# Selective scan: x·dt spread over the scan's partitions by one bf16 product of three stacked parts, and the inputs' front half moved an iteration ahead

## The reference

```python
u = lax.conv_general_dilated(x, conv_kernel, ...); u = silu(u)      # 3 taps, per channel
Bcoeff, Ccoeff = jnp.split(u @ W_bc + b_bc, 2, axis=-1)             # 16 each
dt = log1p(exp((u @ W_dt + b_dt) @ W_dtp + b_dtp))
alpha = jnp.exp(jnp.einsum('dn,bld->bldn', -jnp.exp(A_log), dt))
beta = jnp.einsum('bln,bld,bld->bldn', Bcoeff, x, dt)
_, hs = lax.associative_scan(_scan_op, (alpha, beta), axis=1)       # h = alpha*h + beta
y = jnp.einsum('bln,bldn->bld', Ccoeff, hs) + x * Dcoeff
```

## Time and profile before

| | before |
|---|---|
| median of 3 runs | 1733.51 us |
| the profiled execution, and its span | 1730.11 us, 1728.4 us |
| TensorE matmul busy | 1512.6 us (88%) |
| VectorE, ScalarE, GpSimd busy | 968.1, 763.4, 360.1 us |
| the scan's part of the span | about 1014 to 1404 us |
| granted TensorE clock, whole span | 0.881 |

### The profile page before, as it was taken

How to read it: one execution, slowest core, us unless ns; L and a number is a source line. 1 busy time by engine, 2 the same in 40 slices (tenths; PEclk the granted TensorE clock), 3 DMA queues, 4 the chain that set the end, 5 groups by cost and what they waited for, 6 DMA issues and landing times. The chain is left out here.

```text
span 1728.4 us, 24373 instructions
## 1 busy us (share of the span) xinstructions
PE 1512.6 (88%) x7922; PEld 806.6 (47%) x7922; DVE 968.1 (56%) x1959; ACT 763.4 (44%) x1346; POOL 360.1 (21%) x459
## 2 busy tenths in 40 slices
PE   3984899999999697799999948888989869999998
PEld 2761222323322475577777632222222236777776
DVE  4664788888886266522222643767676755122236
ACT  0210588888888221344343414444444314434442
POOL 2004222222120100300000013556555630000000
PEclk9995799999999798599999976777676758999999
DMA  4002122121220000100000000000000000000001
GB/s 84 1 1 73 54 68 66 40 71 65 74 75 12 1 1 1 16 15 15 14 1 14 1 1 1 1 1 0 0 0 1 1 14 15 1 15 15 15 7 43
DMA packets 56880, 38.45 MB, mean 22 GB/s; under 512 B 16780, under 2 KB 53464, under 8 KB 56792
## 3 DMA queue, kind: packets, MB, share of 16 engines
q1 hardware_dynamic: 54672, 37.04, 7.5%
q10 hardware_dynamic: 2120, 0.28, 0.1%
HBM read 22.23 MB, written 14.68 MB: 21 GB/s over the span
## 5 line engine op out<-in xcount | busy, mean ns | idle before, releaser
L1258 ACT ACTIVATE m_hidden<-m_pU,m_up_b 128x512 f32<-128x512 f32 x320 | 219.9, 687 | 272.3 <-PE m_pU L1395 272.0
L1013 DVE TENSOR_REDUCE at_nm<-at_mx 128x2 f32<-128x1024 f32 x256 | 303.1, 1221 | 45.6 <-PE at_mx L857 44.3
L1402 PEld LDWEIGHTS m_pD<-m_down,m_hidden 128*128 128x128 f32 x2560 | 296.9, 192 | 33.5 <-issue 33.5
L1402 PE MATMUL m_pD<-m_down,m_hidden 128*128 128x128 f32 x2560 | 297.1, 275 | 0.0
L1395 PE MATMUL m_pU<-m_xT_all,m_up 128*128 128x512 f32 x640 | 291.8, 602 | 1.1 <-PEq L1094 1.1
L959 ACT ACTIVATE at_probs<-at_ring 128x512 f32<-128x512 f32 x512 | 268.2, 601 | 45.3 <-PE at_ring L869 44.5
L1371 DVE TENSOR_TENSOR m_out_b<-m_pD,m_down_b 128x512 f32<-128x512 f32 x64 | 44.2, 691 | 283.4 <-PE m_pD L1402 283.4
L1604 POOL TENSOR_TENSOR ss_hc<-ss_h,ss_c_all 128x512 f32<-128x512 f32 x128 | 162.0, 1268 | 154.3 <-DVE ss_h L1826 144.4
L1662 PE MATMUL ss_pA<-ss_dt_of,ss_spread 32*128 32x512 f32 x256 | 150.1, 891 | 33.7 <-DVE ss_h L1826 33.4
L857 PE MATMUL at_mx<-at_kk,at_qq 48*128 48x512 bf16 x512 | 158.2, 399 | 23.7 <-DMA at_kk<-k_stack 13.4
L1395 PEld LDWEIGHTS m_pU<-m_xT_all,m_up 128*128 128x128 f32 x640 | 118.2, 194 | 124.0 <-issue 123.8
(11 more groups left out here) (241 smaller groups left out, 1648.5 us busy)
## 6 DMA issues: line engine op xcount, KB each, us to landing
at_qq<-q_stack SPq DMA_DIRECT2D x64, 96.0 KB, 2.3
at_kk<-k_stack SPq DMA_DIRECT2D x64, 96.0 KB, 2.3
q_stack<-at_qs SPq DMA_DIRECT2D x8, 384.0 KB, 2.6
k_stack<-at_ks SPq DMA_DIRECT2D x8, 384.0 KB, 3.0
X<-in_L_attn_x_dram SPq DMA_DIRECT2D x8, 256.0 KB, 5.5
q_stack<-at_qs SPq DMA_DIRECT2D x8, 256.0 KB, 2.9
k_stack<-at_ks SPq DMA_DIRECT2D x8, 256.0 KB, 3.1
at_qq<-at_ms SPq DMA_DIRECT2D x128, 3.0 KB
```

What stands on the lines that cost most here:

```text
L1013: dve.tensor_reduce(nm[group % 2][:, 2 * half:2 * half + 2, 2 * (pair % 2) + parity], mx[parity][:, :, :], AX.X, ALU.max, negate=True).the ...
L1258: act.activation(hidden[t % 2][:, k, :], pU[k][:, :], ACT.Gelu, bias=up_b[buf][:, k:k + 1]).then_inc(s.gelu_done, 1)
L1402: last = pe.matmul(pD[t % 2][:, c, :], hidden[t % 2][:, k, c * P:(c + 1) * P], down[buf][:, k, :], start=(k == 0), stop=(k == NI - 1))
```

## The change

1. The fp32 x·dt (`xdt`, now one buffer) is taken apart into three bf16 parts that add up to it: high = bf16(xdt) on ScalarE, rest = xdt - high on GpSimd, mid = bf16(rest) on ScalarE, low = rest - mid on GpSimd. SyncE copies the parts by 12 DMAs of 32 partitions x 512 into `stack`, where the three parts of one tile lie on partitions 0 to 95. `spread_xdt` is then one bf16 product with 96 rows.
2. The dt spread stays an fp32 product with 32 rows, whose weights are now called `q.spread32`.
3. pX has three banks and pA three (before two and four). x·dt is spread for n+2, dt for n+1, in this order (before dt for n+2, then x·dt for n+1).
4. The order by hand is new. xT, u, bc and lin of a sequence run at n = 7, 9, 12, 14 of the step before (`front`), b and c at 2 and 3 (`back`), y at 4, the last round of `older` at 1. GpSimd's four operations for dt and x·dt are at 1, 3, 4, 5, the split at 6 to 8, the DMAs at 10.
5. The hardware loop is gone; all ten steps are written out.

```diff
@@ scan_weights, make_scan_constants
-        spread=sb("ss_spread", [P, ROUNDS, DG, NS]), ...
+        spread32=sb("ss_spread32", [P, ROUNDS, DG, NS]), spread=sb("ss_spread", [PARTS * 32, ROUNDS, DG, NS], BF16),
+    pool.tensor_copy(q.spread[:, :, :, :], q.spread32[0:PARTS * 32, :, :, :])
@@ selective_scan, SyncE
+            def stack_parts(b):
+                sp.wait_ge(s.split, b + 1)
+                if b > 1:
+                    sp.wait_ge(s.xdt_bcast, NS * (b - 1))
+                for part in range(PARTS):
+                    for t in range(TILES):
+                        sp.dma_start(stack[b % 2][32 * part:32 * part + 32, t, :], parts[32 * t:32 * t + 32, part, :]
+                                     ).then_inc(stack_in[b % 2], 16)
@@ GpSimd
+                if n == 6:
+                    pool.wait_ge(s.high, b + 1)
+                    pool.tensor_tensor(rest[:, :], xdt[:, :], parts[:, 0, :], ALU.subtract).then_inc(s.rest, 1)
+                if n == 8:
+                    pool.wait_ge(s.mid, b + 1)
+                    pool.tensor_tensor(parts[:, 2, :], rest[:, :], parts[:, 1, :], ALU.subtract).then_inc(s.split, 1)
@@ TensorE
-            def spread(b, par, n, source, banks, done):
-
-                t, r = n % TILES, n // TILES
-                rows = slice(32 * t, 32 * t + 32)
-                pe.matmul(banks[n % len(banks)][:, :], q.spread[rows, r, :, :].rearrange("c d n -> c (d n)"),
-                          source[par][rows, :], start=True, stop=True).then_inc(done, 1)
-
-            def spread_dt(b, par, n):
+            def spread_xdt(b, n):
+
+                m = NS * b + n
+                if n == 0:
+                    pe.wait_ge(stack_in[b % 2], 16 * PARTS * TILES * (b // 2 + 1))
+                wait_for(pe, s.beta, m - X_RING)
+                pe.matmul(pX[m % X_RING][:, :], q.spread[:, n // TILES, :, :].rearrange("c d n -> c (d n)"),
+                          stack[b % 2][:, n % TILES, :], start=True, stop=True).then_inc(s.xdt_bcast, 1)
+
+            def spread_dt(b, n):
+                m = NS * b + n
                 if n == 0:
                     pe.wait_ge(s.dt_ready, b + 1)
-                wait_for(pe, s.h_ready, b, n - RING)
-                spread(b, par, n, dt, pA, s.dt_bcast)
+                wait_for(pe, s.h_ready, m - A_RING)
+                rows = slice(32 * (n % TILES), 32 * (n % TILES) + 32)
+                pe.matmul(pA[m % A_RING][:, :], q.spread32[rows, n // TILES, :, :].rearrange("c d n -> c (d n)"),
+                          dt[b % 2][rows, :], start=True, stop=True).then_inc(s.dt_bcast, 1)
@@ ScalarE, back(b, n)
+                if n == 6:
+                    act.wait_ge(s.xdt_ready, b + 1)
+                    ...
+                    act.copy(parts[:, 0, :], xdt[:, :]).then_inc(s.high, 1)
+                if n == 7:
+                    act.wait_ge(s.rest, b + 1)
+                    act.copy(parts[:, 1, :], rest[:, :]).then_inc(s.mid, 1)
@@ VectorE
-                    if new is not None:
-                        inputs(new, par, n)
-                    if n == 8 and older is not None:
+                    if n == 11 and following(new) is not None:
+                        silu(new + 1)
+                    if n == 5 and older is not None:
```

More of the change, by code:

```diff
@@ L1514, in selective_scan @@
     s = record(**{n: sem(f"{tag}_{n}") for n in (
[L1515 to L1518, removed]
+        "var", "rstd", "shift", "xn_ready", "xT_done", "xT_ready", "u_done", "e_ready", "e1_ready", "inv", "us_ready",
+        "bc_done", "bc_ready", "lin_done", "e_dt", "w_ready", "wm_ready", "ln_ready", "r_ready", "nd_ready",
+        "corr_ready", "dt_ready", "dt_bcast", "xdt_ready", "high", "rest", "mid", "split", "b_done", "b_ready", "c_done",
+        "c_ready", "xdt_bcast", "alpha_ready", "beta", "h_ready", "hc_ready", "rounds", "y_taken", "y_done", "x_done",
+        "zeros_made", "a_made")})
+    stack_in = [sem(f"{tag}_stack_in{i}") for i in range(2)]
     with ExitStack() as ctx:
@@ L1535, in selective_scan @@
         edt, w1, wm, lnw, nd, rw, corr = (sb(n, [P, L]) for n in ("edt", "w1", "wm", "lnw", "nd", "rw", "corr"))
-        shift = sb("shift", [P, NB, NC])
-        beta = [sb(f"beta{i}", [P, L]) for i in range(RING)]
+        beta = [sb(f"beta{i}", [P, L]) for i in range(B_RING)]
         h = [sb(f"h{i}", [P, L]) for i in range(HC_RING)]
@@ L1598, in step @@
+            def step(new, old, older):
+                for n in range(NS):
+                    if new is not None:
+                        inputs(new, n)
                     if old is not None:
+                        m = NS * old + n
                         if n == 0:
                             pool.wait_ge(s.c_ready, old + 1)
-                        wait_for(pool, s.h_ready, old, n)
-                        if not (isinstance(old, int) and old == 0 and n < HC_RING):
-                            pool.wait_ge(s.rounds, ROUNDS * old + n // TILES - 1)
@@ L1692, in add_round, with step @@
                 ins.then_inc(s.rounds, 1)
-            def step(new, old, older, par):
-                if new is not None:
-                    last = ("xT", new)
-                else:
-                    last = ("c", old) if old is not None else ("y", older - 1)
+            def step(new, old, older, last):
+                ahead = following(new)
                 for n in range(NS):
@@ L1708, in step @@
                     elif new is not None:
[L1709 to L1712 removed]
+                        spread_dt(new, 0)
+                    if n == 1 and older is not None:
                         add_round(older, ROUNDS - 1)
[L1714 to L1715 removed]
+                    if n == 2 and new is not None:
+                        last = event("b", new, last)
@@ L1716, in step @@
+                    if n == 3 and new is not None:
+                        last = event("c", new, last)
                     if n == 4 and old is not None:
-                        skip_term(old, 1 - par)
-                    if n == 6 and new is not None:
-                        last = event("lin", new, par, last)
+                        skip_term(old)
+                    if n == 4 and older is not None:
+                        last = event("y", older, last)
                     if n in (6, 10, 14) and old is not None:
@@ L1731, in _ @@
-            transpose_x(0, None)
-            over_steps(pe, step)
+                    if n == 7 and ahead is not None:
+                        last = event("xT", ahead, last)
+                    if n == 9 and ahead is not None:
+                        last = event("u", ahead, last)
+                    if n == 12 and ahead is not None:
+                        last = event("bc", ahead, last)
+                    if n == 14 and ahead is not None:
+                        last = event("lin", ahead, last)
@@ L1734, in _ @@
+                return last
+            last = None
+            for name in ("xT", "u", "bc", "lin"):
+                last = event(name, 0, last)
+            for b in range(NB + 2):
+                last = step(b if b < NB else None, b - 1 if 0 < b <= NB else None, b - 2 if b > 1 else None, last)
         @block.scalar
@@ L1809, in _ @@
-            norm(0)
-            copy_x(0, 0)
-            over_steps(act, step)
+                    if following(new) is not None:
+                        front(new + 1, n)
+            for n in range(NS):
+                front(0, n)
+            over_steps(step)
         @block.vector
```

259 lines of the change are left out of this document (124 added, 135 removed).

## The result

| | before | after |
|---|---|---|
| median | 1733.58 us | 1851.47 us (1849.38 to 1852.48) |
| ratio of the runs | | 1.068, 95% interval 1.0661 to 1.0698 |
| span of the profiled execution | 1728.4 us | 1850.7 us |
| TensorE matmul busy | 1512.6 us | 1656.3 us |
| granted clock, whole span | 0.881 | 0.834 |

The change costs 118 us. I had forecast 1776, with a range up to 1806: the direction was right, the size was not, and the true time lies above even the slow-clock rival.

The account below looks back on a forecast made before the run. TensorE's work and clock bound the scan stage. Seven steps x 5.3 = 37, start +4, end +2: +43 on 1730.1 gives 1773, and the median lies 3.4 above: 1776 us. Range 1708 to 1806; forecast alone 1748 to 1800.

Parts of the forecast that it names:

- One spread of a pair is all but free today, and the change replaces that one.: TensorE's dt and x·dt spreads run side by side, 1.06 us a pair; the change makes the free one cheaper.
- 1.33 us an iteration: TensorE's two spreads, 1.06 + 0.27 at full clock; 16 of them make 21.3 of a step's 34.3 us.
- At the same stretch 34.3 x 1.36: TensorE's work in a scan step, stretched by today's clock factor 1.36: 46.7 us busy.
- rival C: Slower TensorE clock with less of the array in use: stretch 1.5, step 52.5 us, +77, 1810 us; chance 0.10.
- B and C: Their TensorE spreads in a step: c loses its neighbour, +1.0 us at full clock; b may still pair, 0.
- Idle, 1.5 us a step: TensorE's idle time in a scan step: 1.5 us left of today's 4.8, making a step 48.2 us.
- Beta's wait moves to alpha: VectorE's beta no longer waits for x·dt; its 110.6 us of waiting move to alpha, waiting for dt.
- The split, the start: Split and DMAs hidden in a step; at the start open, first scan some 10 us later, net +4, 0 to +8.
- The end: Last sequence, no inputs beside it: 36.6 us against 34.2 today, +2 us.
- Rival A: TensorE with fewer holes stays at 2.4 GHz: step 38.3 us against 42.9, -32, 1702 us; chance 0.22.
- Rival B: The 96-row product overlaps or slips into TensorE's idle time: step 43.2 us, +6, about 1740 us; chance 0.15.
- D: Stack DMAs land behind iteration 14, so TensorE stands still once a step: 2 to 5 us more, 1790 to 1810; chance 0.03.

Follow-up runs that it names:

- e2: The kernel before with only its x·dt product replaced by a 96-row bf16 one from a constant tile, no split or DMAs; 1797.31 us, ratio 1.0388.
- e9: The change with us, the add to X, bc, lin and ScalarE's bc copy one iteration later, products untouched; 1795.95 us, ratio 1.0357.
- e3: The change with the dt product made 128 rows high, weights zero outside the 32 rows that count; 1685.32 us, ratio 0.9742.
- e1: The change's order and rings, but x·dt spread as before by a 32-row fp32 product, without split or DMAs; 1704.91 us, ratio 0.984.
- e10: The change with its events of full height put side by side, products untouched; 1803.09 us, ratio 1.041.
- e5: The change with x·dt cut to one bf16 part over 32 rows, chosen to lie beside the dt products; 1722.57 us, ratio 0.9947.

## Why the prediction was wrong in size

- *One spread of a pair is all but free today, and the change replaces that one.* Right. 2.0 us for a pair at half clock became 2.54, 1.06 became 1.36.
- *1.33 us an iteration, and 34.3 us of TensorE work a step at full clock.* Right within 0.03 per iteration; with 1.36 it is 34.8.
- *"At the same stretch 34.3 x 1.36".* **This is the step that failed.** The busy time of a step was 59.9, so the stretch was 59.9 / 34.8 = 1.72. I took the clock of the old mix of work for the new one. "I expect no more full clock than today" named the direction and gave it no number; rival C, with 1.5, had a chance of only 0.10 and still fell short. The missing 13 us a step (59.9 - 46.7) would be 92 over seven steps; the first two steps and the last were shorter, so the seven steps came out 63 us above my 37. The profiled execution lies 79 above my 1773, and the other 16 are the start and the end.
- In the old order the same term would nearly have held: e2 was busy 48.2 us a step where I had 46.7, and its 1797 us lies in the range. What I had not seen at all is that order and product act together on the clock. "Only 4.8 us of a step are left for a better order to win on TensorE" has the same fault: e9 cut a step from 61.2 to 52 us by the order, 1.5 us of it idle time.
- Of the signs that I had named for being right, the price of an iteration, beta's wait and the first scan came out; TensorE's busy time (45 to 48 us a step) and the clock (0.65 to 0.75) did not.
- *B and C.* Right: at 1.2 GHz one still starts beside a dt product (1304.82 and 1304.83), the other stands alone and takes 1.85 us (1309.23 to 1311.08).
- *Idle, 1.5 us a step.* 1.49 (61.39 - 59.90).
- *Beta's wait moves to alpha.* Right, 110.6 to 19.7 us, and alpha's 199.2. The waits before us and X were named, but they were 8 us each. I had them at 1 to 3 us at full clock and none at half; e3, nearly all at full clock, has 2.9 and 3.3, so it is the half clock that was wrong.
- *The split, the start.* Hidden in a step. SyncE's issues were dearer than thought, 7.57 us for twelve instead of 5.4, and TensorE never waits for them in the scan. The first scan began at 1068.1 where I had 1066. But the split is not the reason: e1, which has none, begins its first scan at 1067.05, and e2, in the old order, at 1052.96. It is the order, with the next sequence's convolution and projections ahead of the first spreads, that makes the start late; the split adds 1.1 us at most. The order's own cost there, +10.8 us in e1, came out near the "some 10 us" that I had put down to the stacks.

```profile
1052.27 7.57 SPq L1584 DMA_DIRECT2D ss_stack<-ss_parts  x12
...
1068.11 1.22 DVE L1865 TENSOR_TENSOR_SCAN ss_h<-ss_pA,ss_beta 128x512 f32<-128x512 f32 x1 [2.07 <-ACT ss_pA L1839]
```

- *The end.* I had +2, and the last sequence's scans alone take 11.1 us more. The sum had the wrong stretch here too: TensorE's clock was 0.50 over them, against 0.62 before.
- *Rival A*, that a TensorE without holes keeps 2.4 GHz, is refuted by e9's steps, busy throughout at 0.56 to 0.71. The Trainium skill's advice (TensorE: Matmul & The Clock Gate, Why this matters for your kernels) to keep TensorE busy without idle gaps is thus not enough here. *Rival B*, overlap of 96 rows with 32, is refuted by the timeline. *C* had the right term and too little of it, and its reason, less of the array in use, does not explain e9 and e10, where the products are the same. *D* did not occur.

## What to carry to other kernels

Before making a TensorE product cheaper, look whether it already runs beside another one: two starts 0.01 us apart mean that its price is next to nothing (a pair took 1.06 us, and the change's dt product alone takes 1.05, from 1338.33 to 1339.38). Where the granted clock in a stage is well below 1.00, the clock is a term of the sum that the change moves, with the mix of products and with their order, and it wants a range of its own; here it moved by more than the work did. A small product padded with zero weights to the full height can be the faster one: e3 is 166 us faster than the change, and 20 us faster than e1, which has the same order with pairs. And when order and product are changed together, time each alone, since here one was worth -26 us by itself and +54 beside the other.

## What the runs showed of the hardware that I had not expected

- An fp32 product made four times as high, with zero weights in the added rows, raised the clock that is granted: 0.98 with 128 rows against 0.56 with 32, in the same order of work (e3 and the change). 64 rows gave 0.75, but there the height is not told apart from the rhythm of the steps.
- TensorE can be occupied without a hole for 260 us and be granted 0.64 of its clock on average (e9).
- Alternating a 96-row bf16 product with a 32-row fp32 one costs 0.27 us an iteration over the same 96-row product with an fp32 one of 128 rows (1.36 against 1.09 at 2.4 GHz).
- Where the bf16 product has 32 rows, two whole iterations, four products, run side by side in 2.24 us at 1.2 GHz (e5), hardly more than one takes.
- Steps of the same instructions can settle in a repeating pattern, 61.39 us alike to the hundredth, 11 us longer than the step ahead of them, and shifting five events by one iteration breaks it.
